# Variance of the patches on ScalarE, one up part and one weighting moved, and all orders rewritten

## The reference, cut to what matters

```
p  = img2patches(x)                               # 1152 x 768
h  = layernorm(p) * g1 + b1                        # mean and variance over 768
h  = layernorm(h @ W + b) * g2 + b2                # 768 -> 192
a  = attention(_layernorm(h))                      # 12 heads of 16, over the 32 images;
                                                   # q and k normalised, logit scale, softmax
h2 = h + a @ out_w.T + out_b
y  = quant(rmsnorm(_layernorm(h2)) * g_in)  @ ternary(w_in).T    # 192 -> 1024: up and gate
z  = silu(gate) * up                                             # 512
out = h2 + quant(rmsnorm(z) * g_out) @ ternary(w_out).T          # 512 -> 192
```

## Time and profile before

| | us |
|---|---|
| median of 3 runs (124.97 to 126.7) | 126.46 |
| the profiled execution, its own time | 125.48 |
| its span, first to last instruction | 123.7 |
| TensorE busy | 115.2 (93%) |
| VectorE busy | 104.4 (84%) |
| ScalarE busy | 79.0 (64%) |
| GpSimd busy | 74.4 (60%) |
| spare products (126 matmul instructions, 63 calls) | 19.2 |

### The profile page before, as it was taken

The page is one execution under the profiler, slowest core; times in us unless marked ns, Lnnn a source line. Parts: engine busy times, 40 slices in busy tenths (PEclk is TensorE's granted clock), DMA queues, the critical chain, the costliest instruction groups (busy, mean ns, idle before and its releaser), DMA issues.

```text
span 123.7 us, 4897 instructions
## 1 busy us (share of the span) xinstructions
PE 115.2 (93%) x1948; PEld 94.5 (76%) x1948; DVE 104.4 (84%) x338; ACT 79.0 (64%) x179; POOL 74.4 (60%) x172
## 2 busy tenths in 40 slices
PE   6999999999999999799999979999999999999960
...
DVE  0399994999999997699997999999999999998810
ACT  0405347774998465583856848677679588999730
POOL 7100357565337460183781877998887999999800
PEclk9999999999999999999999999999999999999999
DMA  3999979899900000000000000000000000111111
GB/s 85 257 194 182 205 113 185 154 194 228 313 4 5 0 0 5 5 5 0 3 5 0 5 0 5 0 5 5 0 5 3 5 0 21 43 44 43 51 53 50
DMA packets 24509, 7.68 MB, mean 62 GB/s; under 512 B 20579, under 2 KB 23909, under 8 KB 24486
## 3 DMA queue, kind: packets, MB, share of 16 engines
...
## 4 chain that ended last, share of the span: by engine, by line
PE 60%; DVE 16%; POOL 9%; issue 5%; DMA 3%; ACT 3%; SPq 0%; DVEq 0%; POOLq 0%
PE bank L750 11%; PE bank L772 8%; PE bank L773 7%; PE bank L796 6%; PE bank L654 5%; PE bank L784 5%; DMA w_emb_sb<-in_L_tok_W_dram 3%; POOL yw L449 3%; PE bank L730 2%; PE bank L761 2%; PE bank L813 2%; DVE bst L951 2%; PE bank L814 2%; DVE yy L893 1%; PE bank L740 1%
## 5 line engine op out<-in xcount | busy, mean ns | idle before, releaser
L654 PE MATMUL bank<-ones 128*128 128x128 f32 x126 | 19.2, 284 | 0.0
L750 PE MATMUL bank<-w_emb_c,xT 128*128 128x192 f32 x108 | 19.2, 328 | 0.0
L750 PEld LDWEIGHTS bank<-w_emb_c,xT 128*128 128x128 f32 x108 | 17.3, 190 | 0.1
L654 PEld LDWEIGHTS bank<-ones 128*128 128x128 f32 x126 | 16.2, 191 | 1.0 <-issue 0.9
L381 POOL TENSOR_TENSOR rs<-mv,mhalf 128x1 f32<-128x1 f32 x9 | 5.2, 588 | 14.8 <-DVE mv L957 14.8
L772 PE MATMUL bank<-w_qkv,xhT 97*128 97x384 f32 (+1 forms) x36 | 12.0, 415 | 0.9 <-DVE qkp L1026 0.8
L773 PE MATMUL bank<-w_qkv,xhT 96*128 96x384 f32 (+1 forms) x36 | 11.7, 405 | 0.0
L449 POOL TENSOR_TENSOR yw<-yy,gout_bc 128x512 f32<-128x512 f32 x8 | 10.2, 1272 | 0.2 <-POOL yy L438 0.2
L403 POOL TENSOR_TENSOR rw<-ssm,ry 128x24 f32<-128x24 f32 x9 | 2.3, 254 | 12.5 <-DVE ry L1000 12.5
L796 PEld LDWEIGHTS bank<-vx,pT 32*32 32x32 f32 x864 | 8.4, 104 | 1.6 <-issue 1.1
L796 PE MATMUL bank<-vx,pT 32*32 32x17 f32 x864 | 9.2, 180 | 0.2
...
## 6 DMA issues: line engine op xcount, KB each, us to landing
...
```

The source lines that it names most:

```text
L654: nc.tensor.matmul(bank[b][:, 3 * P:4 * P], ones[:, :], ones[:, :], start=True, stop=True)
L750: mm = nc.tensor.matmul(emb_bank, xT[:, t % 3, P * k:P * (k + 1)], w_emb_c[:, 3 * (k % 2) + k // 2, :], start=(k == 0), stop=(k == KF - 1))
```

## The change

The variance of tiles 3 to 8 no longer comes from VectorE. ScalarE's copy `xp_` also accumulates the sum of the 768 pixels (`sx1`); GpSimd turns it into minus the mean (`nm1_`); ScalarE squares the copied tile with that bias and accumulates (`xsq_`); GpSimd adds epsilon and divides (`ve1_`), and `rs1_` goes on as before. Tile 4's up part is copied by ScalarE and multiplied by GpSimd; tile 7's weighting goes from GpSimd to VectorE. All four lists are new; TensorE's has 74 calls of `spare` instead of 63 and otherwise the same calls. SyncE's list is unchanged.

```diff
-VAR_ON_DVE = tuple(range(T))
+VAR_ON_DVE = (0, 1, 2)
+VAR_ON_ACT = (3, 4, 5, 6, 7, 8)
-WEIGHED_ON_DVE = (8,)
-WEIGHED_ON_POOL = (0, 1, 2, 3, 4, 5, 6, 7)
-UP_COPIED = (0, 1, 2, 3)
-UP_READ = (4, 5, 6, 7, 8)
+WEIGHED_ON_DVE = (7, 8)
+WEIGHED_ON_POOL = (0, 1, 2, 3, 4, 5, 6)
+UP_COPIED = (0, 1, 2, 3, 4)
+UP_READ = (5, 6, 7, 8)
...
             def rs1_(t):
-                pool.wait_ge(mv1_ok, t + 1)
+                if t in VAR_ON_DVE:
+                    pool.wait_ge(mv1_ok, VAR_ON_DVE.index(t) + 1)
+                else:
+                    pool.wait_ge(ve1_ok, VAR_ON_ACT.index(t) + 1)
...
+            def nm1_(t):
+                pool.wait_ge(xp_ok, COPIED_ON_ACT.index(t) + 1)
+                nc.gpsimd.tensor_scalar(nm1[:, t, :], sx1[:, t, :], -1.0 / FEAT, None, ALU.mult).then_inc(nm1_ok, 1)
+
+            def ve1_(t):
+                pool.wait_ge(xsq_ok, VAR_ON_ACT.index(t) + 1)
+                nc.gpsimd.tensor_scalar(mv1[:, t, 1:2], sv1[:, t, :], 1.0 / FEAT, LN_EPS, ALU.mult, ALU.add).then_inc(ve1_ok, 1)
...
             def xp_(t):
-                nc.scalar.activation(xp[:, t % 3, :, :, :], x_tile(t), ACT.Copy).then_inc(xp_ok, 1)
+                if t in VAR_ON_ACT:
+                    nc.scalar.activation(xp[:, t % 3, :, :, :], x_tile(t), ACT.Copy, accum_out=sx1[:, t, :]).then_inc(xp_ok, 1)
...
+            def xsq_(t, *freed):
+                act.wait_ge(nm1_ok, VAR_ON_ACT.index(t) + 1)
+                wait_all(act, freed)
+                nc.scalar.activation(xsqj[:, :], x_flat(t), ACT.Square, bias=nm1[:, t, :], accum_out=sv1[:, t, :]).then_inc(xsq_ok, 1)
```

The lists, cut to the parts that the prediction speaks of (each `...` stands for calls left out):

```diff
 GpSimd
-            nv_(1); rs3_(3); nm3_(3); rs1_(5); rs2_(4); hg_(4); rs1_(6); hg_(5); rs2_(5); nw_(2); nv_(2); gsc_(); rs1_(7)
-            nv_(5); rs3_(8); e5_(0); yyp(0); yw_(0); ...
+            whs_(); hg_(2); nm1_(3); nm1_(4); nm1_(5); nw_(0); nv_(0); rs2_(2); ve1_(3); ve1_(4); rs1_(3); hg_(3); nm1_(6)
+            rs3_(2); nw_(1); nv_(1); rs1_(4); rs2_(3); ve1_(5); ve1_(6); rs1_(5); ...
+            ... nv_(5); rs3_(7); e5_(1); nm3_(7); yyp(0); ...
 ScalarE
-            xhTe(0); lse_(); xp_(3); xp_(4); sq_(0); xTel(3); xTeh(3); xhTe(1); xTel(4); xp_(5); vx_(0); ms2_(2); xTel(5)
-            ... yqTe(6); ysq_(8); yqTe(7); yq_(8); yqTe(8); tab_()
+            xp_(3); lse_(); xhTe(0); xp_(4); xp_(5); xTel(3); sq_(0); xTeh(3); xsq_(3); xhTe(1); xTel(4); vx_(0); ms2_(2)
+            xsq_(4, (xsq_ok, 1)); xTeh(4); xTel(5); xp_(6); sq_(1); xTeh(5); vx_(1); woEp_(); xsq_(5); ms2_(3); xhTe(2)
+            xsq_(6, (xsq_ok, 3)); ms2_(4, (ms2_ok, 4)); xp_(7); sq_(2); xTeh(6); xTel(6); pr_(0); vx_(2); xh_(3); absi_()
+            ms2_(5); abso_(); xhTe(3); xp_(8); pr_(1); oTe(0); xTel(7); xh_(4); sq_(3); vx_(3); xTeh(7); xsq_(7); xhTe(4)
+            ... yqTe(5); ysq_(8); yqTe(6); yq_(7); yq_(8); yqTe(7); yqTe(8)
 TensorE
-            ... xTh(2, (xTh_ok, 2)); emb(1, (h0s_ok, 1)); qkvT_(); xhT_(0, (xTh_ok, 3)); emb(2); qkv(0); xTl(3); xTh(3)
-            ... proj(0, (sm_ok, 2)); xTh(7); qkv(3, (qkn_ok, 3)); sc(2, (h2_ok, 1)); xhT_(4); emb(7); pv(1, (vx_ok, 4)); ...
+            emb(1, (h0s_ok, 1)); qkvT_(); emb(2, (h0s_ok, 2)); xhT_(0); xTl(3); qkv(0); xTh(3); xTl(4, (xTl_ok, 4))
+            ... qkv(3, (qkn_ok, 3)); wsum_(); xTh(7, (oT_ok, 1)); xTl(8, (xTl_ok, 8))
+            proj(0); xhT_(4, (xTh_ok, 8)); pv(1); emb(7, (h0s_ok, 7)); sc(2, (h2_ok, 1)); ...
+            ... yqT_(7); ff2(6, (out_ok, 6)); spare(4); spare(4); spare(4); yqT_(8, (yqT_ok, 8))
+            ff2(7, (out_ok, 7)); spare(4); spare(4); spare(4); ff2(8, (out_ok, 8)); spare(4); spare(4); spare(4); spare(4)
 VectorE
-            wrow_(); wneg_(); wv_(); c_row_set(); bst0_(); wc_(); xpd(1); ...
-            ... mx_(2); ss_(3); sm_(2); ssm_(3); rsum_(1); ng_(3); on_(1); ...
-            qs4_(7); yy_(6); out_(1); h2_(8); ax5_(5); bst4_(8); ri5_(5); mv4_(8); out_(2); xc_(8); qs5_(5); ax4_(8)
-            ri4_(8); qs4_(8); yg_(7); yy_(7); out_(3); ax5_(6); ri5_(6); out_(4); qs5_(6); ax5_(7); ri5_(7); qs5_(7)
-            yg_(8); out_(5); yy_(8); ywd(8); ax5_(8); out_(6); ri5_(8); qs5_(8); out_(7); out_(8)
+            c_row_set(); wrow_(); wneg_(); wv_(); bst0_(); mv0_(); biasc_(); wc_(); xpd(1); ...
+            ... rsum_(1); np3_(3); on_(1); qkn_(3); h_(6); kT_(3); mv4_(0); mx_(2); sm_(2); xc_(0); ...
+            ri5_(4); xc_(8); ax4_(8); out_(1); ri4_(8); qs5_(4); qs4_(8); yg_(7); yy_(7); out_(2); ax5_(6); ri5_(5)
+            ywd(7, (yq_ok, 5)); ri5_(6); out_(3); qs5_(5); ax5_(7); qs5_(6); yg_(8); ri5_(7); yy_(8); out_(4)
+            ywd(8, (yq_ok, 6)); qs5_(7); ax5_(8); ri5_(8); qs5_(8); out_(5); out_(6); out_(7); out_(8)
```

More of the change, by code:

```diff
@@ L631, in _ @@
-            ms2_(6); xTeh(7); pr_(1); xh_(4); xTel(7); vx_(3); sq_(3); pr_(2); xhTe(4); wo1_(); oTe(1); ms2_(7); wi1_()
-            xTel(8); xTeh(8); sq_(4); pr_(3); oTe(2); vx_(4); wiE_(); xq_(0); xh_(5); xqTe(0); ms2_(8); xhTe(5); th_(0)
-            xh_(6); sq_(5); vx_(5); upc(0); oTe(3); xq_(1); woE_(); xqTe(1); xhTe(6); pr_(4); th_(1); ysq_(0); sq_(6)
-            vx_(6); upc(1); xh_(7); xq_(2); xhTe(7); xqTe(2); th_(2); xq_(3); oTe(4); pr_(5); upc(2); vx_(7); ysq_(1)
-            sq_(7); pr_(6); xh_(8); ysq_(2, (ysq_ok, 2)); oTe(5); xqTe(3); yq_(0); xhTe(8); oTe(6); th_(3); yqTe(0); upc(3)
@@ L636, in _ @@
-            sq_(8); xq_(4); ysq_(3); xqTe(4); xq_(5); yq_(1); pr_(7); xqTe(5); vx_(8); yqTe(1); th_(4); yq_(2); xq_(6)
-            th_(5); pr_(8); oTe(7); ysq_(4); ysq_(5, (ysq_ok, 5)); xqTe(6); yqTe(2); th_(6); oTe(8); yq_(3); xq_(7); yq_(4)
-            xqTe(7); ysq_(6); yqTe(3); th_(7); yqTe(4); xq_(8); yq_(5); xqTe(8); ysq_(7); yqTe(5); th_(8); yq_(6); yq_(7)
-            yqTe(6); ysq_(8); yqTe(7); yq_(8); yqTe(8); tab_()
+            xp0(0); xp0(1); xp0(2); xTel(0); xTeh(0); xTel(1); xTeh(1); ms2_(0); xTeh(2); xTel(2); tab_(); ms2_(1); qkvE_()
@@ L640, in _ @@
+            ysq_(5, (ysq_ok, 5)); th_(6); oTe(8); yq_(3); xq_(7); yqTe(2); xqTe(7); ysq_(6); th_(7); yq_(4); xq_(8)
+            yqTe(3); xqTe(8); ysq_(7); yqTe(4); th_(8); yq_(5); yq_(6); yqTe(5); ysq_(8); yqTe(6); yq_(7); yq_(8); yqTe(7)
+            yqTe(8)
             store(act, T - 1, (2, 3))
@@ L1099, in yy_, with ywd @@
                 nc.vector.tensor_tensor(out=yy[:, t % 3, :], in0=yg[:, t % 2, :], in1=up_ps[:, :], op=ALU.mult).then_inc(yy_ok, 1)
-            def ywd(t):
-                if t == 8:
+            def ywd(t, *freed):
+                if t == WEIGHED_ON_DVE[0]:
                     dve.wait_ge(ld_gout, 16)
@@ L1152, in _ @@
-            ax5_(2); ri4_(5); ss_(8); qs4_(5); ssm_(8); mx_(7); ng_(8); qs5_(1); ri5_(2); bst4_(6); sm_(7); np0_(8)
-            mv4_(6); np1_(8); qs5_(2); np2_(8); xc_(6); np3_(8); pT_(7); qkn_(8); ax4_(6); kT_(8); qT_(8); yg_(4); rsum_(7)
-            ri4_(6); yy_(4); qs4_(6); mx_(8); on_(7); sm_(8); ax5_(3); yg_(5); pT_(8); yy_(5); ax5_(4); h2_(7); ri5_(3)
-            out_(0); ri5_(4); bst4_(7); rsum_(8); mv4_(7); on_(8); xc_(7); qs5_(3); ax4_(7); qs5_(4); ri4_(7); yg_(6)
-            qs4_(7); yy_(6); out_(1); h2_(8); ax5_(5); bst4_(8); ri5_(5); mv4_(8); out_(2); xc_(8); qs5_(5); ax4_(8)
@@ new lines, in _ @@
+            mv3_(8); ng_(6); mv4_(3); ri4_(2); xc_(3); ax4_(3); np0_(6); qs4_(2); np1_(6); ri4_(3); np2_(6); rsum_(4)
+            np3_(6); on_(4); qkn_(6); mx_(5); qT_(6); sm_(5); kT_(6); yg_(1); ax5_(0); pT_(5); ss_(7); mx_(6); ssm_(7)
+            sm_(6); ri5_(0); ng_(7); rsum_(5); qs4_(3); on_(5); pT_(6); h2_(4); yg_(2); np0_(7); bst4_(4); np1_(7)
+            rsum_(6); mv4_(4); np2_(7); on_(6); np3_(7); xc_(4); qkn_(7); ax4_(4); qT_(7); h2_(5); qs5_(0); bst4_(5)
+            kT_(7); mv4_(5); yg_(3); xc_(5); ri4_(4); ax4_(5); qs4_(4); ri4_(5); ss_(8); qs4_(5); ssm_(8); h2_(6); ng_(8)
```

127 lines of the change are left out of this document (68 added, 59 removed).

## The result

The changed kernel took **126.69 us** (median of 20 runs, 125.32 to 128.4), the kernel before 126.65 (20 runs, 124.61 to 132.28). The ratio is **1.0094, 95% interval 1.006 to 1.0129**: slower by 0.9%. Equal medians and a ratio above 1 stand together because the ratio leaves out the slow runs of either kernel, and in the 23 runs of the kernel before beside e1, where the clock is on record, 14 of the 15 slow ones had lost some of TensorE's clock. The profiled execution of the changed kernel took 126.58, its span is 124.5; forecast were 125.8 and 124.0.

The account below looks back on a forecast made before the run. Bounds: TensorE to about 50 us, VectorE to tile 4's output, then the store queue. Tile 4's first store at 112.5 plus 11.5 gives span 124.0, time 125.8 (own range 124.3 to 127.5; 8 in 10: 123.2 to 128.4).

Parts of the forecast that it names:

- Up to the scores of tile 2: TensorE's new order: `qkv(0)` late, net +0.75, four more steps before `sc(2)`, +3.7; `mx_(2)` moves from 47.29 to 51.7.
- Variance on ScalarE: Takes some 6.5 us off VectorE, mostly between 22 and 45 where TensorE is full: no kernel time by itself.
- VectorE from there: VectorE from `mx_(2)` to the end of `qs5_(8)`: 62.6 us instead of 69.7, ending at 114.3.
- the prediction's own cuts (3.8 and 1.1): VectorE after `mx_(2)`: 3.8 us less work with overlap, 1.1 less because `np3` no longer meets GpSimd's `yyp`.
- the 2.2 of dropped waits: VectorE after `mx_(2)`: waits of 1.6 (`rsum` for `pv(1)`) and 0.6 (`yg` for `th`) were to go.
- The tail: Store queue: `out_(4)` ends at 112.5, 1.0 later; span ends 11.5 us after tile 4's first store, at 124.0.
- Swaps at nothing: Tile 4's up part and tile 7's weighting: exchanged products cost VectorE and GpSimd nothing; ScalarE gains about 0.6 us.
- Eleven spares: TensorE: added spare products, at most 0.30 each, 3.3 us, fall in its waits of the last 30 us.
- I keep 125.8: Forecast time kept, though its base, the profiled 125.48, is low against the median 126.46 of the runs shown.
- freed VectorE time is real: Rival: VectorE's 6.5 us come through, span 120.2, time 122.0; half of it gives 123.9. Chance 0.20.
- The ScalarE gate: Rival, 24 to 50 us: squares delay copies TensorE needs; 3.7 us reaching `sc(2)` gives 129.5, two thirds 128.3. Chance 0.18.
- The shared interface: Rival: GpSimd's large products hold VectorE's two-input steps; price 0.6 to 1.7, time 126.4 to 127.5. Chance 0.12.

Follow-up runs that it names:

- e1: Changed kernel with the last two store chunks of tiles 6 and 7 moved from SyncE's queue to ScalarE's: 124.6 us, 0.9918 of before.
- e3: Changed kernel with the variance of tiles 3 to 8 back on VectorE, new orders kept: 128.33 us, 1.0201 of before.
- e5: Changed kernel with GpSimd's last 23 small operations in another order: 126.71 us, 1.0109 of before.
- e7: Changed kernel with four stores moved to ScalarE's queue, GpSimd's tail reordered, and outputs of tiles 4 and 5 earlier: 125.72 us, 1.0016 of before.
- e9: e7 with GpSimd's tail reordered again, `e5_(8)` ahead and `an5_(6)`, `f2_(6)` behind `s5_(8)`: 125.41 us, 0.9949 of before.
- e11: Changed kernel with tile 4's product `yy_(4)` back on VectorE: 126.58 us, 1.0063 of before.
- e10: Changed kernel with tile 7's weighting `yw_(7)` back on GpSimd, behind `f_h_(8)`: 127.87 us, 1.0103 of before.
- g1: Changed kernel measured again, nothing altered: 126.32 us, 1.0087 of before.
- e4: Kernel before with its old orders, but the variance of tiles 3 to 8 on ScalarE: 134.36 us, 1.0603 of before.
- g2: Kernel before with three spare products in TensorE's hole at 51 us and four stores moved to ScalarE's queue: 125.82 us, 1.0021 of before.

## Why the prediction was wrong

The profiled execution took 0.8 us more than the forecast 125.8: 0.5 in the span (124.5 for 124.0), 0.3 between span and time. The prediction put the change 0.3 above its own base of 125.48 and called that no change; measured is a loss of 0.9%.

- **Up to the scores of tile 2: right, with a wrong detail.** `mx_(2)` was forecast at 51.7 and came at 51.17. The copy `xp_(3)` was to wait for data that "lands at 21.52, whatever stands before it"; it ran at 20.68 without a wait, so `qkv(0)` came at 22.28, not 22.95, without the gap ahead of it. The earlier trace rows gave the landing of one execution, and I took it for fixed. In the trace of the changed kernel the last piece of that group landed at 20.42; what brought it forward no run shows.
- **Variance on ScalarE, "no time of the kernel by itself": mis-sized.** TensorE is full up to 50, as argued, but e3 puts about 1.3 us on it.
- **"VectorE from there": the step that failed.** 62.6 us were forecast from `mx_(2)` to the end of `qs5_(8)`; it took 115.99 - 51.17 = 64.8. VectorE's work was nearly right: it is busy 60.77 us in this stretch, after 65.35 before, where the prediction's own cuts (3.8 and 1.1) leave 60.45. Its idle time was not: 4.05 us, where 4.33 before less the 2.2 of dropped waits leave 2.1. The waits that went were replaced by others: 1.54 for `s5_` (0.4 before), 0.73 for `rsum_(4)` behind TensorE's hole in `pv(4)` and 0.53 for a `proj`. All waits of 0.15 and more in the stretch come to 3.3 us, over the 3 that the prediction had named as a sign of being wrong. I counted VectorE's work and dropped old waits, but did not lay GpSimd's new order beside it at the end, where the earlier trace rows had shown GpSimd at 16.88 of 18: the engine with no room was the one whose small operations I left out of the sum. That these operations are what VectorE waits for is in the trace; no reordering (e5, e7, e9) took the waits for GpSimd away, so what the step would have been worth with GpSimd in the sum stays an argument. The hole in `pv(4)` could not be forecast from the rows.
- **The tail: "as long as the outputs of tiles 5 to 8 come within that time" failed.** `out_(5)` waits for `qs5_(8)` and ended at 116.32 instead of 114.8, so the queue stood empty for 1.25 us before tile 5, and the span is 8.15 behind the first store of tile 5, not 11.5 behind the first of tile 4. My estimate from these: with tile 4's stores out of the way and `out_(5)` at 114.8, 8.15 us behind it give a span of 123.0, less than the 123.7 before, so the 2.2 us missed on VectorE are enough to turn a gain into a loss. `out_(4)`, forecast at 112.5, came at 113.36.
- **That the span was only 0.5 off is luck.** Tile 4's stores began 0.9 later than forecast and the queue idled for 1.25, but the 1.49 us issue of the earlier trace rows did not recur, so the 18 issues took 8.4 us instead of 9.6, and the last one stood 1.5 ahead of the end instead of 1.9: 0.9 + 1.25 - 1.2 - 0.4 = 0.5. e1 confirms the queue as the end: four issues less gave about 2 us.
- **Swaps at nothing.** e11 agrees. e10 leans to 1 us more for the old place of `yw_(7)`, on GpSimd again.
- **Eleven spares "in TensorE's waits of the last 30 us": half wrong.** Behind 94 us there are five spares more than before (44 for 39); three of the others stand between 57 and 76 us (10 for 7). Taking out all ten of that stretch gives 0.4 to 0.7 where the clock holds, so they cost time, and they buy the clock.
- **"I keep 125.8."** 125.48 came from an execution at clock 1.0, and most runs of the kernel before are not: the changed kernel's median is level with the other's only because it holds the clock. Its own loss with the clock held is 1.1 to 1.3 us: 1.1 between the two profiled executions, 1.2 by the ratio, and on g1's chip 126.32 (clock 0.991 to 1.0) against 124.98, the median of the seven runs of before at 0.998 or more.
- **Rivals.** That freed VectorE time is real was partly so (e3). The ScalarE gate did not close: no wait of TensorE from 20 to 50. It closed in e4. The shared interface held GpSimd and not VectorE: `e5_(6)` and `s5_(7)` took 0.85 us longer together, ahead of `s5_(8)`. In e5 these delays were smaller and `qs5_(8)` came no earlier, so that they reach the time is not shown.

Left open: how much of e1's gain the hole in `pv(4)` and the chips' spread carry, and which other hole takes g2's clock in four of twelve runs.
